# Gate logits from raw rows, normalisation on ScalarE and a changed combination in a perceiver block

## The reference

```python
x = x + cross_attention(layernorm(x), ctx_768)       # 16 heads, 257 keys of 192 channels
x = x + recurrent_attention(layernorm(x))            # below
x = x + mixture(layernorm(x))                        # below

# recurrent_attention: time t looks at earlier times s < t
scores  = tanh(inputs @ W) @ proj
context = softmax(where(s < t, scores, min)) @ inputs
out     = tanh(concat(inputs, context) @ concat_w.T + concat_b)
out[:2] = inputs[:2]                                 # the first two times keep the normed rows

# mixture: 8 experts, the two best of a token are used
gate = softmax(x @ Wg.T); top2, renormalised
out  = sum over experts e of comb[e] * ((a * sigmoid(b)) @ Wo.T + bo),  [a, b] = x @ W1[e].T + b1[e]
```

## Time and profile before

| | |
|---|---|
| median of 3 runs | 626.54 us (625.04 to 626.72) |
| profiled execution | 622.39 us |
| its span, first to last instruction | 620.6 us |
| mean granted TensorE clock | 0.991 of 2.4 GHz |
| busy: TensorE, VectorE, ScalarE, GpSimd | 595.0, 461.0, 335.3, 321.9 us |

### The profile page before, as it was taken

The page is one execution under the profiler, slowest core; times in us unless marked ns, Lnnn a source line. Parts: engine busy times, 40 slices in busy tenths (PEclk is TensorE's granted clock), DMA queues, the critical chain, the costliest instruction groups (busy, mean ns, idle before and its releaser), DMA issues. The chain is left out here.

```text
span 620.6 us, 21697 instructions
## 1 busy us (share of the span) xinstructions
PE 595.0 (96%) x8364; PEld 482.7 (78%) x8364; DVE 461.0 (74%) x1081; ACT 335.3 (54%) x735; POOL 321.9 (52%) x474
## 2 busy tenths in 40 slices
PE   8999999999999999999999999996899999998886
PEld 3788878888788887888887688883578888884665
DVE  4687877888678886777777675999789987773553
ACT  3677868878687786788766156541122333330221
POOL 3357858787578777678874311111333333314761
PEclk9999999999999999999999999996999999999999
DMA  8624543776355845774400795119534433434774
GB/s 230 171 64 115 165 162 108 245 175 207 113 189 156 217 149 170 198 232 152 146 4 3 314 407 232 35 35 360 196 128 140 137 128 127 132 124 131 226 238 118
DMA packets 65205, 102.10 MB, mean 165 GB/s; under 512 B 15409, under 2 KB 42097, under 8 KB 64081
## 3 DMA queue, kind: packets, MB, share of 16 engines
q1 hardware_dynamic: 59808, 86.42, 43.3%
q0 software_dynamic: 4432, 13.50, 7.9%
q10 hardware_dynamic: 864, 0.79, 0.5%
HBM read 69.42 MB, written 31.26 MB: 162 GB/s over the span
## 5 line engine op out<-in xcount | busy, mean ns | idle before, releaser
L537 DVE TENSOR_SCALAR Pm<-scores 128x514 f32<-128x514 f32 x128 | 88.1, 688 | 57.2 <-PE scores L750 57.1
L653 ACT ACTIVATE Pm<-Pm,nm 128x257 f32<-128x257 f32 x256 | 115.8, 506 | 2.5 <-DVE nm L542 2.5
L542 DVE TENSOR_REDUCE nm<-Pm 128x2 f32<-128x514 f32 x128 | 87.5, 684 | 2.2
L1623 POOL DMA_INDIRECT Xg<-y_d,inv x39 | 37.2, 954 | 87.5 <-PE scores L1810 70.8
L648 ACT ACTIVATE PT<-bank 128x512 f32<-128x512 f32 x64 | 38.3, 598 | 75.2 <-PE bank L761 75.2
L731 PE MATMUL bank<-hA,wH 128*128 128x258 f32 x256 | 75.3, 305 | 0.1
L738 PE MATMUL bank<-wH,hA 128*128 128x256 f32 x256 | 74.2, 301 | 0.5 <-DVE PT L549 0.5
L761 PE MATMUL bank<-cst,Pm 128*128 128x128 f32 x512 | 70.0, 279 | 0.0
L731 PE MATMUL bank<-hA,wL 128*128 128x258 f32 x256 | 69.2, 281 | 0.0
L738 PE MATMUL bank<-wL,hA 128*128 128x256 f32 x256 | 68.9, 280 | 0.0
L1825 PE MATMUL bank<-W,xh 128*128 x208 | 66.7, 401 | 1.3 <-DVE xl L1733 1.3
(11 more groups left out here) (261 smaller groups left out, 1425.7 us busy)
## 6 DMA issues: line engine op xcount, KB each, us to landing
w_d<-whl SPq DMA_DIRECT2D x64, 256.0 KB, 3.4
W<-w_d SPq DMA_DIRECT2D x8, 2048.0 KB, 15.6
g_d<-gg SPq DMA_DIRECT2D x39, 256.0 KB, 2.4
wst<-in_W1T SPq DMA_DIRECT2D x32, 256.0 KB, 3.7
cx<-in_ctxT SPq DMA_DIRECT2D x31, 258.0 KB, 2.9
cx<-in_ctxT SPq DMA_DIRECT2D x62, 129.0 KB, 3.4
bb<-in_b SPq DMA_DIRECT2D x8, 512.0 KB, 12.8
xb<-in_x SPq DMA_DIRECT2D x4, 512.0 KB, 4.9
```

The costliest lines, as they stand in the source:

```text
L537: v.tensor_scalar(Pm[:, i % 2, 2 * p:2 * p + 2, :], S4[:, 2 * p:2 * p + 2, 0:NK], -CLAMP, CLAMP, ALU.max, ALU.min).then_inc(s_cl, 1)
L542: v.tensor_reduce(nm[:, i % 2, 2 * p:2 * p + 2], Pm[:, i % 2, 2 * p:2 * p + 2, :], AX.X, ALU.max, negate=True).then_inc(s_nm, 1)
L653: a.activation(Pm[:, i % 2, g, :], Pm[:, i % 2, g, :], ACT.Exp, bias=nm[:, i % 2, g:g + 1]).then_inc(s_ex, 1)
L1623: g.indirect_dma_start(out=Xg[:, i % 3, :], out_offset=None, in_=y_d, in_offset=bass.IndirectOffsetOnAxis(ap=inv[:, i:i + 1], axis=0)).the ...
```

## The change

The gate. `lifted` transposes the raw rows of `xb`, two tiles to a bank, as soon as `third` has written them. `gated` takes them as weights and moves the gate's eight columns, so that the logits come out with tokens on partitions; in chunk 0 it also multiplies ones with the gate's weights, which gives each expert's sum of weights (`s8`). `best` subtracts mean times that sum. The scale `rs` is left out until the third block, where the differences to the best logit are multiplied by it ahead of the exponentials (the order of a token's logits doesn't depend on it). `gate_out`, `turned_back`, VectorE's `gate_in` and `final_norm` go.

Normed and kept rows. All of `yn` is normed by ScalarE, behind `outs`. `kept` goes to ScalarE too, as the last step of passes 0 to 3: xb = ka * xb + kb, with ka = 1 + m10 * rs and kb = m10 * nb made by GpSimd (`keep`). On TensorE `rank(2)` moves behind the loop, and two waits ahead of the filling matmuls go. SP no longer waits for the kept rows.

The combination. The two gathered rows of a tile have semaphores of their own; `fo` has a buffer for each tile; at the end the products of the last tiles stand in another order between the transposes.

```diff
 # SP, second block
 def store_y(c):
-    sp.wait_ge(f_yn, min(2 * c + 2, 7))
-    sp.wait_ge(f_yv, 2 * c + by_vector(c))
+    sp.wait_ge(f_yn, 4 * c + 4)
...
     store_y(3)
-    sp.wait_ge(u_b2, 4)
 # TensorE
 def lifted(c):
-    for h in range(2):
-        b = take("t3", c, h)
-        for j in range(4):          # waits for yn's rows, f_yv or f_yn
-            mm = t.transpose(b[:, 128 * j:128 * j + 128], yn[:, j, 128 * h:128 * h + 128], ident)
+    for p in range(2):
+        b = take("t3", c, p)
+        t.wait_ge(u_x3, 2 * c + p + 1)
+        for h in range(2):
+            for jj in range(2):
+                o = 256 * h + 128 * jj
+                mm = t.transpose(b[:, o:o + 128], xb[:, 4 * c + 2 * p + jj, 128 * h:128 * h + 128], ident)
         mm.then_inc(f_t, 1)
 def gated(c):
     b = take("g", c)
-    for h in range(2):
-        for j in range(4):          # after a wait for gh
-            mm = t.matmul(b[32 * j:32 * j + 32, 0:128], WgT[:, h, :], gh[:, h, 128 * j:128 * j + 128], ...)
+    if c == 0:
+        for h in range(2):
+            t.matmul(b[:, 64:64 + E], cst[:, C_ONE:C_ONE + 128], WgT[:, h, 0:E], ...)
+    for p in range(2):
+        t.wait_ge(f_hi, 2 * c + p + 1)
+        for jj in range(2):
+            o = E * (2 * p + jj)
+            for h in range(2):
+                x = 256 * h + 128 * jj
+                mm = t.matmul(b[:, o:o + E], gh[:, p, x:x + 128], WgT[:, h, 0:E], ...)
     mm.then_inc(f_gm, 1)
...
     if k == 5:
         take("idle")
-        t.wait_ge(u_z, 8)
         busy(2)
-        t.wait_ge(f_mv, 16)
-        busy(1)
-        rank(t, 2, take("r", 2))
...
-    if 0 <= k - 2 < 4:
-        turned_back(k - 2)
+rank(t, 2, take("r", 2))
+busy(2)
 slots(t, 2)
 # VectorE
 def best(c):
-    v.wait_ge(f_g, c + 1)
-    v.tensor_copy(gl[:, k, :], bank("g", c)[:, 128:256]...)
+    if c == 0:
+        v.wait_ge(f_gm, 1)
+        v.tensor_copy(s8[:, :], bank("g", 0)[:, 64:64 + E]).then_inc(f_s8, 1)
+        v.wait_ge(f_s8, 1)
+    v.wait_ge(f_mv, 4 * c + 4)
+    v.tensor_tensor(um[:, :, :], bc(mv[:, k, 0]), s8[...], ALU.mult).then_inc(f_um, 1)
+    v.wait_ge(f_um, c + 1)
+    v.wait_ge(f_gm, c + 1)
+    v.tensor_tensor(gl[:, k, :], bank("g", c)[:, 0:4 * E]..., um[:, :, :], ALU.subtract).then_inc(f_gl, 1)
...
-    if k < 4:
-        kept(k)
-    if 0 <= k - 2 < 4:
-        final_norm(k - 2)
-    if k == 5:
-        gate_in()
 # GpSimd
+def keep(c):
+    g.wait_ge(u_rs, c + 1)
+    g.tensor_scalar(ka[:, k], rs[:, k], m10, 1.0, ALU.mult, ALU.add).then_inc(u_k, 1)
+    g.tensor_scalar(kb[:, k], nb[:, 0, k], m10, 1.0, ALU.mult, ALU.mult).then_inc(u_k, 1)
+    g.wait_ge(u_k, 2 * c + 2)
 # ScalarE
+def kept(c):
+    a.wait_ge(u_k, 2 * c + 2)
+    a.wait_ge(u_xn, 4 * c + 2)
+    for n in range(4 * c, 4 * c + 4):
+        a.activation(xb[:, n, :], xb[:, n, :], ACT.Identity, bias=kb[:, n:n + 1], scale=ka[:, n:n + 1]).then_inc(u_b2, 1)
...
     exps(k - 1)
-    final_norm(k - 2)
     normed(k + 1)
     gate_in(k - 2)
     weights(k - 1)
-    gate_out(k - 2)
     outs(k - 1)
+    final_norm(k - 2)
+    kept(k)
 # third block, VectorE
-v.tensor_tensor(gs[:, 1, :], g8[:, :, 1], g8[:, :, 0], ALU.subtract).then_inc(f_gs, 1)
-v.tensor_tensor(gl[:, :, :], gl[:, :, :], g8[:, :, 0]..., ALU.subtract).then_inc(f_gs, 1)
+link(v.tensor_tensor(gs[:, 1, :], g8[:, :, 1], g8[:, :, 0], ALU.subtract))
+v.tensor_tensor(gs[:, 1, :], gs[:, 1, :], rs[:, :], ALU.mult).then_inc(f_gs, 1)
+link(v.tensor_tensor(gl[:, :, :], gl[:, :, :], g8[:, :, 0]..., ALU.subtract))
+v.tensor_tensor(gl[:, :, :], gl[:, :, :], rs[:, :]..., ALU.mult).then_inc(f_gs, 1)
...
-    v.wait_ge(c_g[j % 4], 32 * (j // 4 + 1))
+    v.wait_ge(c_g[0][j % 4], 16 * (j // 4 + 1))
     v.tensor_scalar(zc[:, j % 2, :], cg[:, j % 4, 0, :], cmb[:, 0, j:j + 1], ...)
     v.wait_ge(c_m, j + 1)
+    v.wait_ge(c_g[1][j % 4], 16 * (j // 4 + 1))
 # third block, TensorE
-back(0)
-for j in range(NTILE):
-    if j + 1 < NTILE:
-        back(j + 1)
-    product of tile j, four parts
+back(0)
+for j in range(NTILE - 3):
+    back(j + 1)
+    product(j, range(4))
+product(NTILE - 3, range(4))
+back(NTILE - 2)
+product(NTILE - 2, range(2))
+back(NTILE - 1)
+product(NTILE - 2, range(2, 4))
+product(NTILE - 1, range(4))
```

More of the change, by code:

```diff
@@ L960, in build @@
             if k == 5:
-                uses += [(("idle",), u_o, 8), (("r", 2), u_rk, 3)]
+                uses += [(("idle",), u_o, 8)]
             if 0 <= k - 2 < 4:
@@ L1186, in gated @@
                     b = take("g", c)
-                    for h in range(2):
[L1188 to L1193, removed]
-                        for j in range(4):
-                            mm = t.matmul(b[32 * j:32 * j + 32, 0:128], WgT[:, h, :], gh[:, h, 128 * j:128 * j + 128],
-                                          start=(h == 0), stop=(h == 1), skip_group_check=True)
+                    if c == 0:
+                        for h in range(2):
+                            t.matmul(b[:, 64:64 + E], cst[:, C_ONE:C_ONE + 128], WgT[:, h, 0:E],
+                                     start=(h == 0), stop=(h == 1), skip_group_check=True)
+                    for p in range(2):
[4 more added lines that the diff above has]
+                                x = 256 * h + 128 * jj
+                                mm = t.matmul(b[:, o:o + E], gh[:, p, x:x + 128], WgT[:, h, 0:E],
+                                              start=(h == 0), stop=(h == 1), skip_group_check=True)
                     mm.then_inc(f_gm, 1)
-                def turned_back(c):
-                    t.wait_ge(f_gc, c + 1)
-                    t.transpose(bank("g", c)[:, 128:256], gc[:, :], ident).then_inc(f_g, 1)
                 def busy(n):
@@ L1287, in normed @@
                                         ALU.subtract, ALU.mult).then_inc(u_xv, 1)
[L1289 to L1298, removed]
-                def gate_in():
-                    v.wait_ge(f_t, 8)
-                    v.wait_ge(f_gm, 3)
-                    v.tensor_copy(gh[:, 1, :], bank("t3", 3, 1)[:, :]).then_inc(f_hv, 1)
-                def kept(c):
-                    if c == 0:
-                        v.wait_ge(u_xv, 2)
-                    v.wait_ge(u_xn, on_scalar(c))
-                    v.scalar_tensor_tensor(out=xb[:, 4 * c:4 * c + 4, :], in0=xn[:, :, :], scalar=m10,
-                                           in1=xb[:, 4 * c:4 * c + 4, :], op0=ALU.mult, op1=ALU.add).then_inc(u_b2, 1)
                 def values(c):
@@ L1464, in final_norm @@
                     if c:
-                        a.wait_ge(f_t, 2 * c)
                         a.wait_ge(f_yd, 16 * c)
-                    for j in range(by_vector(c), 4):
+                    for j in range(4):
                         n = 4 * c + j
@@ L1470, in final_norm @@
                                      scale=rs[:, n:n + 1]).then_inc(f_yn, 1)
+                def kept(c):
+                    a.wait_ge(u_k, 2 * c + 2)
+                    if c == 0:
+                        a.wait_ge(u_xv, 2)
+                    a.wait_ge(u_xn, 4 * c + 2)
+                    for n in range(4 * c, 4 * c + 4):
+                        a.activation(xb[:, n, :], xb[:, n, :], ACT.Identity, bias=kb[:, n:n + 1], scale=ka[:, n:n + 1]
+                                     ).then_inc(u_b2, 1)
                 def squashed(c):
@@ L1514, in gate_in @@
                 def gate_in(c):
-                    for h in range(2 - (c == 3)):
+                    for h in range(2):
                         a.wait_ge(f_t, 2 * c + h + 1)
@@ L1583, in build @@
         e_gd = [sem("e_gd0"), sem("e_gd1")]
-        c_g = [sem(f"c_g{i}") for i in range(4)]
+        c_g = [[sem(f"c_g{k}{i}") for i in range(4)] for k in range(2)]
         c_z = sem("c_z")
@@ L1590, in build @@
         c_f = sem("c_f")
-        c_out = [sem(f"c_out{i}") for i in range(4)]
+        c_out = sem("c_out")
         def tb(i):
@@ L1851, in _ @@
                         t.wait_ge(c_f, j - 3)
-                    for m in range(4):
+                    for m in part:
                         mm = t.matmul(B[4 + j % 4][:, 0:C], zT[:, j % 2, 128 * m:128 * m + 128], WoT[:, m, :],
                                       start=(m == 0), stop=(m == 3))
-                    mm.then_inc(c_o, 1)
+                    if m == 3:
+                        mm.then_inc(c_o, 1)
+                back(0)
[8 more added lines that the diff above has]
+                product(NTILE - 1, range(4))
 def bcast(ap, n):
```

77 lines of the change are left out of this document (37 added, 40 removed).

## The result

The changed kernel took 638.25 us in the median of 4 runs (636.38 to 640.88), the kernel before 626.63 us beside it (625.04 to 628.11): ratio 1.0185, interval 1.015 to 1.022, so 11.6 us slower. The forecast was 5.3 us slower. The profiled execution is the longest of the four, 640.88 us with a span of 639.1; that of before was a short one, 622.39. Their spans differ by 18.5 us, and some 7 us of that is the choice of executions.

The account below looks back on a forecast made before the run. TensorE's queue sets the pace from 373 to 418 us, VectorE's to the routing, GpSimd's gathers in the combination. +4.5 + 3.0 - 0.95 + 2.0 - 3.2 = +5.3 us, so 631.9 us; range 625.5 to 637, the forecast's own 629 to 635.

Parts of the forecast that it names:

- Stops of TensorE, +4.5: Attention passes: rows moved to ScalarE delay the tanh, so TensorE stops 1.3, 0, 1.4 and 1.8 us ahead of logits.
- Rival A: ScalarE in the passes: the rows fit beside the tanh, TensorE never stops, the 4.5 goes, 627.4 us; chance 0.16.
- The clock should hold: TensorE in the stops ahead of the logits: the granted clock stays 1.00, as over 572 to 574 us.
- Gate pairs, +3.0: Gate on TensorE: 16 instructions with full-width fp32 loads take 1.74 us instead of 0.80, 0.11 a step; +3.0 us in all.
- VectorE's end, -0.95: 418 to 439 us: VectorE loses normed rows and a copy, gains small operations; index row inv 0.95 us sooner.
- rival B: Gate on TensorE: the pairs are short, 0.046 us each, 3.3 us less, 628.6 us; chance 0.16.
- First gather and SP's queue, +2.0: End of the second block: late store and weight loads make the first gather wait 1.0 us and land slower; +2.0 us.
- Combination, -3.2: Combination's gathers and last products: separate semaphores and a new order at the end save 3.2 us.
- steady part, -2.2: Combination's gather steps: a semaphore for each row set brings transposes 0.5 us sooner, most waits go; -2.2 us.
- The end, -1.0: After the combination's last gather: earlier first product and reordered last products save 1.0 us.
- Rival C: First gather: it lands behind the biases as store_y(3) did behind the experts, +5 us, 636.9 us; chance 0.10.

Follow-up runs that it names:

- Gate alone: Only the change of gate and routing, against the kernel before, with kept rows, final rows and combination as before: 629.18 us, ratio 1.0036.
- Turned round: Gate alone with the gate's matmuls back to standing 32-column weights, gate_out and turned_back, still on raw rows: 626.13 us, ratio 0.9999 to the kernel before.
- the run alone: The kernel before with only the three alterations of the combination: 626.40 us, ratio 0.9983.
- the turned gate: Gate-only kernel with the gate's matmuls back the old way round, here with the combination's three alterations added: 626.44 us, ratio 0.9994 to the kernel before.

## Why the prediction was wrong

The direction was right, and so were the terms of the stops and of the gate. Two terms were mis-sized, the queue's by 2.9 us and the combination's by 2.1 to 3.2 (it measured between -1.1 and nothing), which makes 5 to 6 of the 6.3 us between forecast and result.

- **Stops of TensorE, +4.5:** right. 0.63, 0, 1.57 and 1.98 us in the trace (the first is half of its 1.3, because ScalarE began the rows of pass 1 at 355.84 and not at 357.00); without the kept rows ahead of the tanh the time falls by 4.4. Rival A (the rows fit beside the tanh) is wrong for the eight rows of a pass, and right for four: these took 2.07 us, under the bound that the rival named, and with either kind placed elsewhere 0.62 us at most is left of the stops. "The clock should hold" was wrong in the profiled execution, where it fell in the longest stop and cost some 2 us, and right in two others with a stop of 1.96 and 1.97 us. I had weighed that stop against one stretch of the trace where it held; nothing here tells beforehand which it will be.
- **Gate pairs, +3.0, and VectorE's end, -0.95:** right. 1.78 us for 16 is 0.111 us a pair; rival B's 0.046 is out. By the Trainium skill (TensorE: Matmul & The Clock Gate, LDWEIGHTS) the load of 128 columns is an estimated 107 ns; the trace agrees within 4%. Gate alone: 2.3 for a forecast of 2.05. Turned round: 2.3 back. From the last outs to VectorE's last operation in the block it is 11.96 us instead of 13.31, and from the third block's start to inv 0.39 us more: -0.96.
- **First gather and SP's queue, +2.0: the step that failed.** It measured 4.9 (1.0116 less 1.0037, of 626.5 us; 5.4 in the traces). The late loads were seen, and put at 2.9 us. The prediction let inv be done when VectorE is, 0.95 us sooner than before, and the first gather wait for the landing of store_y(3); it put the issue of SP's bias loads at nothing. Missed were three things: final_norm(3) waits for the late store of chunk 2 (2.28 us); SP is not through with the five bias loads until some 11 us after it issued the weights, and the third block of every engine stands behind that, so that inv comes 10.3 us late and releases the first gather in place of a landing; and the wait for this gather's rows lets the clock fall for the first list (1.6 us). I reckoned with when transfers land, and not with when the queue that issues them is through.
- **Combination, -3.2: the other step that failed.** Its steady part, -2.2, came from the stops of one execution. In four traces with the old combination the 32 gathers span 42.6, 46.5, 46.5 and 48.2 us, in ten with the new one 45.6 to 47.5; the one read for the prediction was the shortest of all. The end, -1.0, may hold: from the last gather 13.7 us in the mean of the four (13.2 to 14.5), 12.6 of the ten (11.3 to 14.1). Both parts together, from the first gather to the end, take 59.7 and 59.2 us in the mean. By the run alone it is -1.1, with the turned gate -0.3, neither told from zero.
- **Rival C**, the first gather behind the biases, 636.9 us, came nearest in time, but not by its price: that gather took 5.9 us from issue (449.16) to the transposes, near the 5.0 taken and not 10. The Trainium skill (DMA: Bandwidth & Descriptors, Issuing engines are not separate DMA queues) lets transfers of all queues interleave on the same 16 engines. The traces can't tell whether the gather interleaved or came last: the engines were full until some 452 us, and its rows were used at 455.03, behind that.

4.4, 4.9 and the 2.3 of the kernel with both kinds of rows moved make 11.6, but by construction: each is the difference between one run and the next. The traces give a second measure that leaves the combination out, from where TensorE gets to the logits of pass 1 (their start less the stop ahead of them) to the first gather of the combination, 359.90 to 579.25 in the changed kernel:

| trace | us |
|---|---|
| the kernel before, two traces; with the new combination | 204.6, 204.2; 204.1 |
| gate alone | 206.7 |
| both kinds of rows placed elsewhere | 207.2 |
| only the final rows placed elsewhere | 207.6 |
| only the kept rows placed elsewhere | 212.6 |
| the changed kernel; with four matmuls in the stop | 219.4; 217.3 |

To the 2.9 us with both moved, the kept rows alone at the end of the pass add 0.4 us, the final rows alone 5.4 (the queue), and both 12.2. What both cost beyond that, 6.4 us, is in the main the stops of passes 3 and 4 and what the clock lost in the last, and these come only when both kinds stand ahead of the tanh. How the loss is shared between the two kinds of rows therefore depends on which is moved first.

The rows well placed and the combination are worth nothing together (1.0037 with both, 1.0036 with the gate alone). Which engine is held in the combination's waits of 2 us and more stays open, as does the 2.6 us by the medians between moving the final rows alone and both, of which the traces show 0.4.

## What to carry to other kernels

When work moves to an engine that is half idle, look for the instruction that it will stand ahead of: 28 rows cost 9.4 us at the end of ScalarE's pass and next to nothing at two other places of it, and either kind of them alone would have all but fitted ahead of the tanh. When a store comes late, follow the whole queue that issues it, to the block's end, and expect that taking one of several waits of like size may gain nothing. A gain that is read from the stops of a single execution needs a second trace of the same kernel first.

## What the hardware showed

The issue of a transfer can itself take microseconds. The five bias loads of 512 KB each took SP 3.14 us where the DMA engines had stood idle (weight loads ahead of the store, DMA share 0.02 and less in the 3 us before), 2.65 to 3.72 us in eight traces where they went out 6.9 to 8.1 us behind two weight loads of 2 MB, and 6.00 to 7.15 us in four where they went out 5.5 us behind them. In all twelve of these the issue ended 10.4 to 12.7 us after the weights'.

TensorE's granted clock fell to 0.50 in a stop of 1.98 us between busy passes, and stayed at 1.00 through stops of 1.96 and 1.97 us at the same place in two other executions, and through those of 1.57 us a pass earlier: the same stop can cost some 2 us or nothing. And the gathers of one and the same program took 42.6 us in one execution and 46.5 in another.
